# Attention, two-way Mamba and routed feed-forward in one kernel: second SBUF inputs taken off VectorE, and a new order of the work

## What is computed

```python
def reference(x, ...):
    x = x + attention(x)                    # 1024 x 1024 scores, softmax, one head of 128
    t = tokens(x)
    h = layernorm(t)
    m = mamba(h, forward) + mamba(h, backward)
        # in_proj; conv over 4 taps; silu; x_proj -> dt, B, C; dt = softplus(...)
        # 16 states x 256 channels: h = exp(dt*A)*h + dt*B*x ; y = sum h*C
        # y = (y + x*D) * silu(z) ; out_proj
    t = t + m + w2 @ leaky_relu(w1 @ (layernorm(m) * ln_g + ln_b) + b1, 0.01) + b2
    n = layernorm(t)
    w = n @ wr                              # one weight per token
    t += n ; for the 511 heaviest of 1024 tokens also  t += w * ffn(n)    # 512 hidden, gelu
    return from_tokens(t)
```

## Time and profile before

| | |
|---|---|
| runs | 8608.84, 8619.99, 8632.47 us; median 8619.99 |
| profiled execution: its own time | 8629.83 us |
| its span | 8628.1 us |
| mean granted TensorE clock | 0.978 of 2.4 GHz |
| one image in the loop (64 steps) | 261.56 us |

### The profile page before, as it was taken

One profiled execution on the slowest core, in us unless ns is written; L12 is line 12 of the kernel. 1 busy time (PEld: TensorE's weight loads), 2 busy tenths in 40 slices (PEclk: granted clock), 3 DMA queues, 4 the chain that ended last, 5 costly groups with the idle time before them and its releaser, 6 DMA issues. The chain is left out here.

```text
span 8628.1 us, 152387 instructions
## 1 busy us (share of the span) xinstructions
PE 7996.8 (93%) x53760; PEld 6192.3 (72%) x53760; DVE 7505.7 (87%) x10155; ACT 7333.3 (85%) x12894; POOL 7292.5 (85%) x5965
## 2 busy tenths in 40 slices
PE   6899999999999999999999999999999999999987
PEld 4777777777777777777777777777777777777765
DVE  3888998888998889998889899889988889998886
ACT  3888888888888888988888888889888889888875
POOL 2889888888888888888888888888888989888985
PEclk8999999999999999999999999999999999999998
DMA  1222222222222222222222222222222222222221
GB/s 41 72 65 77 73 73 74 64 72 75 72 75 68 68 73 75 75 71 70 66 73 75 73 73 67 71 71 76 73 70 66 76 70 75 75 72 65 76 71 37
DMA packets 321380, 604.48 MB, mean 70 GB/s; under 512 B 40961, under 2 KB 43714, under 8 KB 320578
## 3 DMA queue, kind: packets, MB, share of 16 engines
q1 hardware_dynamic: 320578, 594.31, 22.3%
HBM read 556.42 MB, written 20.97 MB: 67 GB/s over the span
## 5 line engine op out<-in xcount | busy, mean ns | idle before, releaser
L1049 POOL TENSOR_TENSOR g<-h,c_all 128x1024 f32<-128x1024 f32 x2048 | 4977.7, 2431 | 669.6 <-DVE h L1143 485.6
L841 ACT ACTIVATE da<-dt,a_neg 128x512 f32<-128x512 f32 x4096 | 2777.0, 712 | 117.7 <-DVE h L1143 114.1
L1143 DVE TENSOR_TENSOR_SCAN h<-da,h,ps 128x512 f32<-128x512 f32 x2048 | 2553.9, 1269 | 249.6 <-PE ps L511 113.4
L1143 DVE TENSOR_TENSOR_SCAN h<-da,ps 128x512 f32<-128x512 f32 x2048 | 2432.3, 1209 | 319.0 <-PE ps L511 191.4
L511 PE MATMUL ps<-ident,ub 128*128 128x128 f32 x16384 | 2410.9, 278 | 317.1 <-DVE h L1143 200.6
L511 PEld LDWEIGHTS ps<-ident,ub 128*128 128x128 f32 x16384 | 1896.5, 142 | 1039.4 <-issue 545.3
L853 ACT ACTIVATE ub<-u_tok,b_tok 128x256 f32<-128x256 f32 x5120 | 2247.9, 497 | 131.2 <-PE ps L511 60.8
L515 PE MATMUL ps<-ident,g 128*128 128x128 f32 x16384 | 2284.1, 275 | 7.3 <-POOL g L1049 7.3
L515 PEld LDWEIGHTS ps<-ident,g 128*128 128x128 f32 x16384 | 1907.9, 142 | 459.3 <-issue 448.9
L1035 POOL TENSOR_SCALAR ub<-u_tok,b_tok 128x256 f32<-128x256 f32 x3072 | 1539.8, 511 | 398.6 <-DVE u_tok L1231 211.7
L830 ACT ACT_TABLE_LOAD x476 | 610.7, 1283 | 8.5
(11 more groups left out here) (123 smaller groups left out, 9269.2 us busy)
## 6 DMA issues: line engine op xcount, KB each, us to landing
c_all<-c_rows SPq DMA_DIRECT2D x2048, 256.0 KB, 3.2
x_in<-in_x SPq DMA_DIRECT2D x32, 512.0 KB, 5.2
t_old<-t SPq DMA_DIRECT2D x32, 512.0 KB, 3.2
out<-tile_b SPq DMA_DIRECT2D x32, 512.0 KB, 4.1
c_rows<-rows SPq DMA_DIRECT2D x128, 32.0 KB, 2.8
w_conv<-in_conv_rows SPq DMA_DIRECT2D x1, 512.0 KB
f_w<-in_f_w SPq DMA_DIRECT2D x2, 256.0 KB
hid<-in_in_proj SPq DMA_DIRECT2D x1, 256.0 KB
```

Of the source, the lines that this page charges most:

```text
L841: act.activation(da[:, n % 2, half, :], dt[:, slot, half, :], ACT.Exp, scale=a_neg[:, r, half, s:s + 1]).then_inc(da_made, 1)
L1049: pool.tensor_tensor(g[:, n % 2, :, :], h[:, n % 2, :, at:at + BANK], c_all[:, n % RING, :].unsqueeze(1).to_broadcast([P, NH, BANK]), ALU.mult
L1143: dve.tensor_tensor_scan(h[:, n % 2, half, at:at + BANK], da[:, n % 2, half, :], ps[:, DB + half, :], before, ALU.mult, ALU.add).then_inc( ...
```

## The change

1. **Taps**: ACT writes tap 4 with bias to PSUM (bank Y+1), DVE adds the three others there, and ACT's silu reads it from PSUM.
2. **dt's maximum** is written to PSUM; u is made from PSUM and xc; ACT then copies dt from PSUM to SBUF (new, `AT_DTKEEP`, 128 x 1024, four per image). PE's transposes of u, and `da` of the next quarter, wait for that copy.
3. **Leaky relu**: ACT writes 0.01 times the value to `hid`; DVE takes the maximum of PSUM plus bias and `hid`. PE's next matmul into these banks waits for DVE instead of ACT.
4. **Ties**: POOL makes `earlier` (tile_a) by one `affine_select`, 128 x 1024 (new, `AT_EARLIER`); DVE's eight `tied` are then tensor_scalars with one input.
5. **Weights**: DVE makes `is_kept`, POOL multiplies by `w_col` (new, `AT_WTIMES`).
6. **First turn**: ACT issues `probs_t` of tile i ahead of `probs` of tile i+1.
7. **Branch hint**: `hint_back_edge=True` on the loop.
8. **Places**: nearly all tables have other numbers.

```diff
-    AT_TAPS = ((31, 31, 34), (90, 98, 99), (155, 155, 155), (210, 214, 219))
+    AT_TAPS = ((27, 29, 29), (79, 84, 84), (152, 155, 156), (219, 220, 222))
-    AT_CSTORE = (44, 97, 179, 220)
+    AT_CSTORE = (32, 110, 158, 239)
+    AT_DTKEEP = (50, 112, 178, 240)
-    AT_RANK = (202, 205, 205, 209, 209, 209, 212, 217)
+    AT_EARLIER = 223
+    AT_RANK = (231, 231, 231, 232, 235, 237, 238, 238)
-    AT_HID = (198, 199, 200, 200, 204, 204, 205, 208)
-    AT_GELU = (201, 203, 205, 207)
+    AT_HID = (225, 225, 228, 228, 231, 233, 235, 235)
+    AT_GELU = (228, 229, 231, 233)
-    AT_FFN = (211, 212, 214, 214, 216, 233, 238, 241)
-    AT_T3 = (224, 245)
-    AT_OUT = 245
-    AT_OUTKEEP = 248
-    AT_STORE = 251
+    AT_FFN = (236, 237, 237, 237, 237, 240, 241, 242)
+    AT_T3 = (242, 246)
+    AT_OUT = 247
+    AT_OUTKEEP = 249
+    AT_STORE = 239
-    FIRST_PTKEEP = tuple(FIRST + 5 + 4 * i for i in range(8))
+    FIRST_PTKEEP = tuple(FIRST + 4 + 4 * i for i in range(8))
...
-                            act.activation(xc[:, slot, 1, :], ps[:, Y + 1, :], ACT.Identity, bias=conv_b[:, r, 1:2],
+                            act.activation(ps[:, Y + 1, :], ps[:, Y + 1, :], ACT.Identity, bias=conv_b[:, r, 1:2],
                                            scale=w_taps[:, r, PAD:PAD + 1]).then_inc(proj_kept, 1)
...
+                        if at == AT_DTKEEP[k]:
+                            act.wait_ge(u_made, since(u_made, prep(k, 1, 1)))
+                            act.activation(dt[:, side, :, :], ps[:, Y:Y + NH, :], ACT.Copy).then_inc(dt_kept, 1)
...
+                            if at == AT_EARLIER:
+                                pool.wait_ge(w_row_kept, since(w_row_kept, 1))
+                                pool.wait_ge(base_made, since(base_made, 2))
+                                pool.affine_select(out=by_block(earlier), in_=by_block(w_row[:, :]), compare_op=ALU.is_gt,
+                                                   fill=LOWEST, base=0, pattern=[[0, NB], [-1, P]], channel_multiplier=1
+                                                   ).then_inc(earlier_made, 1)
+                            if at == AT_WTIMES:
+                                pool.wait_ge(ranked, since(ranked, 1))
+                                pool.tensor_tensor(w_kept[:], is_kept[:], w_col[:], ALU.mult).then_inc(w_kept_made, 1)
...
-                            dve.scalar_tensor_tensor(xc[:, slot, 1, :], x_proj[:, slot % NCH, tap:tap + BANK],
-                                                     w_taps[:, r, tap:tap + 1], xc[:, slot, 1, :],
+                            dve.scalar_tensor_tensor(ps[:, Y + 1, :], x_proj[:, slot % NCH, tap:tap + BANK],
+                                                     w_taps[:, r, tap:tap + 1], ps[:, Y + 1, :],
                                                      ALU.mult, ALU.add).then_inc(tapped, 1)
...
-                            dve.tensor_tensor(u[:], dt[:, side, :, :], xc[:, slot, :, :], ALU.mult).then_inc(u_made, 1)
+                            dve.tensor_tensor(u[:], ps[:, Y:Y + NH, :], xc[:, slot, :, :], ALU.mult).then_inc(u_made, 1)
...
-                            dve.scalar_tensor_tensor(hid[:, o, :], hid[:, o, :], SLOPE, hid[:, o, :],
-                                                     ALU.mult, ALU.max).then_inc(hid1_leaky, 1)
+                            dve.scalar_tensor_tensor(hid[:, o, :], banks(X), b1[:, o:o + 1], hid[:, o, :],
+                                                     ALU.add, ALU.max).then_inc(hid1_leaky, 1)
...
-                            dve.scalar_tensor_tensor(tied[:, j % 2, :], w_row[:, mine], w_col[:, j:j + 1], below[:],
-                                                     ALU.is_equal, ALU.mult, accum_out=heavier[:, 2, j:j + 1]
-                                                     ).then_inc(counted, 1)
+                            dve.tensor_scalar(tied[:, j % 2, :], earlier[:, mine], w_col[:, j:j + 1], None,
+                                              ALU.is_equal, ALU.add, accum_out=heavier[:, 2, j:j + 1]).then_inc(counted, 1)
...
-                            dve.scalar_tensor_tensor(w_kept[:], rank[:], float(KEPT), w_col[:], ALU.is_lt, ALU.mult
-                                                     ).then_inc(w_kept_made, 1)
+                            dve.tensor_scalar(is_kept[:], rank[:], float(KEPT), None, ALU.is_lt).then_inc(ranked, 1)
...
-        with nc.Fori(0, (B - 2) // JOINED) as group:
+        with nc.Fori(0, (B - 2) // JOINED, hint_back_edge=True) as group:
```

More of the change, by code:

```diff
@@ L32, in conv_attn_mamba_mod_kernel @@
     SLOPE = 0.01
+    LOWEST = float(np.finfo(np.float32).min)
     EXP_MAX = float(np.log(1e15))
@@ L837, in decay @@
                         if s == 0 and n >= DS:
-                            act.wait_ge(dt_kept, since(dt_kept, prep(n // DS - 1, NH, half + 1)))
+                            act.wait_ge(dt_kept, since(dt_kept, prep(n // DS - 1, 1, 1)))
                         if now:
```

188 lines of the change are left out of this document (94 added, 94 removed).

## The result

The changed kernel takes **8423.35 us** in the median of four runs (8418.81 to 8431.67), against 8614.42 before. The ratio is 0.978 (95% interval 0.976 to 0.980): faster by 2.2%, where 0.95% was forecast. The profiled execution took 8420.61 us with a span of 8418.8, against 8629.83 and 8628.1.

What follows compares the result with a forecast made beforehand. No single engine bounds the kernel; each block of four steps lasts as long as its most loaded engine. 31 x (-4.2 + 2.2) = -62, -16 and -5 make -83: 8547 us profiled, 8538 as median, range 8420 to 8655.

Steps and rivals of the forecast that it cites:

- no stall: At the store ending an image: C lands in time, -4.2 to -6.7 us per image, 8469 to 8391; chance 0.22.
- -4.2 us per image: Most loaded engines summed over blocks of four steps: operations and places save 4.2 us per image, ends -2.4 and -6.7.
- Second inputs off VectorE: One-input forms on VectorE: 3.3 us less DVE per image, 4.5 less POOL from g's standstill; taps gain little.
- Places: Step tables: two long blocks fall from 22.7 and 22.2 to 14.9 and 13.5 us, steps 56 to 59 rise to 27.4.
- The store: Store moved to slot 239: C's load lands later, g of step 63 starts late, +2.2 us per image, ends 0 and 6.
- Branch hint: At the loop's branch back: 3.5 us less idling before the first scan, five times, -16 us taken, ends -18 and 0.
- Longer waits on banks 4 and 5: u's transposes wait 1.0 us more, W1's second half 1.3; covered by the next scan pair, so taken as 0.
- First turn: Copy probs_t issued ahead of probs: 1.1 us sooner for seven tiles, -5 us in all, ends -7 and +2.
- Is_kept: Expected 0.17 us on DVE; rival beside any other: it still waits for GpSimd, 0.77 us per image, 8562; chance 0.3.
- Slower: SP queue at an image's end: 6.5 us stall per image against 4.2 gained, 8670 us; chance 0.17.
- Eaten by the dense block: Banks 4 and 5 and the dense four steps: two to four us per image more, 8600 us; chance 0.18.
- The hint does nothing: At the loop's branch back, beside any other rival: 16 us more, 8554 us; chance 0.2.

Runs made afterwards that it cites:

- e1_store_251: The changed kernel with only the store of the finished image put back to slot 251: 8301.57 us, ratio 0.962.
- e5_places_alone: The code of the kernel before with all places of the changed kernel, store in slot 251, no hint: 8788.65 us, ratio 1.020.
- e4_ops_alone: The changed kernel's operations, first turn and hint with the places of the kernel before, store in slot 251: 9055.92 us, ratio 1.049.

## Why the prediction was right or wrong

The direction was right, the forecast's own range (8505 to 8580) was missed, and 8423 lies just inside the wide one, by chance: it is near the figure of the rival *no stall*, while the stall was there at twice its size. The profiled execution came out 126 us below the 8547 that the sum gave it: 102 of them in the images (-180 measured, -78 with the hint forecast), 21 in the first turn, 3 at the end.

**The step that failed: "-4.2 us per image" for operations and places.** Measured are -9.7 with the store left late (`e1_store_251`), more than twice as much; with the early store -5.1 are left, where the forecast had -2.0. The price list was not at fault: in the two kernels that were compared, taps went from 758 to 735 ns and nearly all else as forecast. The sum over blocks was. Its first cut gave -6.7, which was passed over for the mean over four cuts. And its pieces do not add up: the four last blocks as listed change by -0.3 and "the other twelve fall by 4 together", which makes -4.3 and not 253.5 - 260.2 = -6.7. In the runs the last four blocks rise by 1.4 us together, and it is the other twelve that carry the gain: 11.1 us (means of undisturbed images, store late), of which steps 36 to 39 have 6.8, steps 28 to 31 have 4.8 and steps 12 to 15 have 2.7. In the kernel before, PE was busy 19.3 of 20.1 us and 19.7 of 20.2 in steps 28-31 and 36-39, at the full clock; the windows are to be set beside those of the late store above (15.38 and 12.87 us):

```profile
2091.57:2111.64 20.07, 19.26 (x141) 15.72 (x139) 18.42 (x22) 16.15 (x29) 12.43 (x11) 1.00 0.26 82
...
2125.82:2146.06 20.24, 19.69 (x117) 13.85 (x116) 17.43 (x22) 18.59 (x36) 19.49 (x16) 1.00 0.13 46
```

The prediction shows its loads for the last four blocks only, so why it gave the others so little stays open.

**Second inputs off VectorE: their worth was read from the wrong schedule.** The durations came out (g 2371, tied 343, leaky 1272, is_kept 176, taps 735). But "The taps gain little: 758 against 740" took the price of the old places for a property of the instruction, and u was not counted. A table of undisturbed images, store late in all:

| | operations of before | new operations |
|---|---|---|
| places of before | 261.2 | 275.9 (269.5 with u and the copy moved) |
| new places | 266.4 | 251.6 |

In the old places a GpSimd instruction was still running at the start of 104 of the 384 taps, and 3 took over 1 us. In the new places it was at 331, and 214 took over 1 us: the same taps cost 1540, and the operations are worth 14.8 us per image, 8.1 by the taps and 2.0 by dt; the 4.7 left (leaky, ties, weights) were not taken apart. The Trainium skill, SBUF — State Buffer, section on who interferes with whom, has it that a VectorE instruction with two SBUF inputs and a GpSimd instruction that reads SBUF exclude one another for the whole instruction; the two taps of 4.75 us around one g of 2.35 agree. The prediction applied that section to `is_kept`, and priced taps and u by their means. So it did not see that the new places pay only with the taps out of SBUF; its sum, which compares the two whole kernels, was not put off by that.

**Places.** The sum of the largest engines was within 1% for both kernels taken whole (253.5 against 251.6 measured, 260 against 261.2), but the change is the difference of the two, where 1.9 and 1.0 us of error weigh. It was the wrong tool for kernels in which an operation stands in a place made for another: for the operations alone it gave 3 to 4 us less, and they took 14.7 more; for the places alone 5.5 less, and they took 5.2 more. It counts work, not chains. It also holds no granted clock and no wandering: steps 50 and 51 took 14.1 us in the mean before and 11.0 in the best images. In the new order the ranking and gelu lie in steps 56 to 59, and these repeat from image to image with a standard deviation of under 0.01 us, at a clock of 1.00 (steps 50 and 51 before: 2.1).

**The store: right mechanism, mis-sized.** +2.2 forecast, 4.6 measured. The landing was right, "about 5.3 us after the store's issue": g started 5.5 behind it. Wrong was the margin, taken over from the old order as 3.2 us from the store's issue to g. In the new order with the late store, g starts at 2144.41 and the copy ends at 2141.88, 2.5 us apart where the old order has 3.4; a store issued 0.2 behind the copy leaves 2.3, and 5.5 - 2.3 is near the 3.13 us that g idles. And the late load of x_in, of which "not all the rest is lost", is a second wait of 1.3 us that appears as soon as the first shrinks. The 512 KB ahead of C's load are one of two causes: with x_in late they could be taken away and 3.3 of 4.6 us stayed, since SP's hold makes x_in late too; with x_in in early they are worth 3.7, and the hold alone 0.8.

**Branch hint.** -16 forecast, 2.7 x 5 = -13 measured. Not forecast: the early store holds the barrier of each round, 6 x 2.5 = +15, which cancels it.

**Longer waits on banks 4 and 5**, taken as 0: right in the new places, wrong as a rule. In the old ones dt's part costs 13 us per image and the wait behind leaky 3.

**First turn.** -5 forecast (ends -7 and +2), -26 measured up to the first scan: outside the ends. The step counted 1.1 us for each of seven tiles at the durations seen; those durations were taken at a lowered clock, which the shorter gap lifts.

**Is_kept.** 176 ns, the optimistic value, but not for the reason given. GpSimd was idle in 31 of its 32 instances, and in these places the old instruction with two inputs takes 168 as well (`w_kept` in `e5_places_alone`). The pessimistic rival had the mechanism right: in the old places (`e4_ops_alone`), where GpSimd's product runs, `is_kept` with its one input takes 375 to 422 ns in 31 of 32 instances, and each time ends some 0.03 us behind the product:

```profile
632.30 1.27 POOL L1083 TENSOR_TENSOR xc<-xc,sz 128x512 f32<-128x512 f32 x1
...
633.18 0.42 DVE L1286 TENSOR_SCALAR is_kept<-rank 128x8 f32<-128x8 f32 x1
```

That a PSUM source costs more did not appear in the taps: 735 against 758.

**The rivals.** *Slower* fell: the stall of 4.6 is just under its point of decision of 4.9, and the gain was more than twice as large. *Eaten by the dense block* fell: it takes 25.7 us, less than its load of 27.4. *The hint does nothing* is what the changed profile seems to say, and is wrong. Two ranges do not follow from their terms, with no effect on the outcome: 2 to 4 us per image more than the forecast are 8600 to 8662, not 8570 to 8630, and a stall of 1 to 4 us gives 8501 to 8594, not 8505 to 8580.

**Its own test** had two halves. An image "over 260 or under 255 us" did not come: 256.5, since two errors of 5.5 and 2.4 us per image had opposite signs. A test of each term by itself, the first block and the rest, would have shown both. "No wait names `c_all`" did come: g's idle time stands as "issue" or for VectorE. That half misled, for with the store late, and nothing else changed, the 3.13 us are gone.

## What to carry to other kernels

The mean duration of an instruction that can be blocked by another engine is a property of the schedule it was measured in: before pricing its removal, look at what else runs beside it in the new order, not in the old. Operations and places that were made for each other can each be harmful alone (here +5.6% per image and +2.0%, and -3.7% together), so a change of both is tried as one and then reduced. Where a forecast is the small difference of two large sums, write down every block of both, and add them up. And ask of every transfer moved up in an in-order queue what its wait holds, at the end of a loop's round too, where it can hide the gain of another edit.

## What the hardware showed that was not expected

- TensorE's clock is part of latency chains: 1.5 us less idling per tile kept the granted clock at 1.00 instead of 0.80, and made a tile of 9.1 us one of 6.5.
- One collision can make a stretch wander: two steps of the old order take 11.0 us, 13.2 where one `tied` of 0.35 us takes 2.53 beside g, and 14.9 or 16.0 where the clock falls after that.
- A taken branch back costs 3.4 us, and 0.5 with the hint (3.8 and 0.6 in the mean of five).
- A VectorE instruction with one SBUF input, `is_kept` over eight elements, takes 172 ns by itself and some 400 where a product of GpSimd is running, ending with it.
- Two VectorE instructions with two SBUF inputs each, 0.74 us by themselves, took 4.75 us next to one g of 2.35 and one `res` of 1.26.
- GpSimd's affine_select over 1024 elements takes 1.09 us, the one over 128 takes 0.28: it is much cheaper for each element than g.
